# Decoder layer on one core: the scan result turned by VectorE blocks and a DRAM scratch, and three passes moved

## The chip, the cores and the metric

The kernel runs on one core of a Trainium2 chip. The metric is the device time of one execution in microseconds. TensorE (PE) multiplies matrices into PSUM, VectorE (DVE) and ScalarE (ACT) do elementwise work, GpSimd (POOL) shares elementwise work, and SyncE (SP) issues DMAs. Each engine works through its own queue in order and waits on semaphores.

## The reference

A post-norm decoder layer for 16 batches of 256 rows and 512 channels:

```python
x = layernorm(x + attention(x))              # 16 heads of 32, low-rank updates in each projection
kv = ctx * ctx                               # k = v = ctx, per channel
r[t] = decay[head] * r[t - 1] + kv[t]        # linear recurrence over the rows
x = layernorm(x + x * r)
h = gelu(silu(bitlinear(x, w1, b1)))         # x quantised to 8 bits, w1 ternary, 512 -> 2048
h = layernorm_2048(h) * ln_g + ln_b
x = layernorm(x + bitlinear(h, w2, b2))      # h quantised, w2 ternary, 2048 -> 512
```

## The kernel before, in words

One body of the loop, `body(j)`, works on four batches at once: the attention of batch j, the LayerNorms 1 and 2 and the up-projection of batch j-1, the middle of the feed-forward of batch j-2, and the down-projection and last LayerNorm of batch j-3. `lead()` fills this pipeline, `drain()` empties it. The order on each engine is written out by hand in five `body(j)` functions, one for each engine; the semaphores count up per batch (`wait(eng, name, b, k)`). A batch has NT = 2 tiles of 128 rows (index q).

- Attention, for head groups c = 0 to 3: `qk` (PE), `qk_hi` (ScalarE, L670), `qk_lo` (VectorE, L979), `scores` (PE, L1358), `maxima` (VectorE, L962 to L972), `shiftT` (PE, L1367, and its copy on ScalarE, L677), `shifted` (PE, L1382, into the four banks of `wave`), `probs_of` (ScalarE, L655), `weighted` (PE), `attn_norm` (VectorE, L986 to L995), `attn_split` (GpSimd, L437 and L440).
- The o product (PE), `layernorm1_sum` (VectorE, L1021), `inverse_std1` (GpSimd), `normalise` (ScalarE, L693).
- The context is loaded with channels on partitions into `ctx_sb` (`load_ctx`, L310), squared on ScalarE (L686, `ctx_square`), and scanned along the rows on VectorE at the end of `body(j)` (`scan`, L1003, clamped by L1006).
- In the next body PE transposes the scan result back to rows on partitions: `r(j, q)`, four 128x128 transposes for each q into a PSUM bank (L1455). `layernorm2_sum` (L1029) reads that bank and the rows. `inverse_std2` and `x_rms` (GpSimd, L462 to L520) and `normalise` follow.
- `quantise_x` (VectorE, L1052 to L1072) and `xq_store` (ScalarE, L702) write `xq`; a DMA transpose (`transpose_x`, L326) makes `xqT`; PE multiplies it in eight products `f(j, u)` (L1467 and, for the bias, L1468) into three banks in turn: `f(j, 3)` takes the bank of `f(j, 0)`, and waits until `silu` (ScalarE, L717) has read it. `gelu` (L723), `h_var` (L733), `h_rstd` (GpSimd) and `h_norm` (L738) follow.
- `g_mul` (GpSimd, L547) multiplies a 128x2048 tile by ln_g, `z_add` (VectorE, L1085) adds ln_b, `z_max` (L1090), `z_square` (ScalarE, L748), `z_rms` (GpSimd, L554, L557), `quantise_z` (VectorE, L1108 to L1117), `zq_store` (ScalarE, L708).
- A DMA transpose (`transpose_z`, L334) makes `hqT`; PE multiplies it in `y(j, q)` (L1474), `layernorm3_sum` (VectorE, L1130), `inverse_std3` (GpSimd, L482 to L487), `normalise`, and `store_out` (L319).

The order on PE around the change is `y(j,1)`, `shiftT(j,2)`, `r(j,0)`, `r(j,1)`, `shifted(j,2)`, `qk(j+1,0)`, `scores(j,3)`, `weighted(j,2)`, and later `qk(j+1,1)`, `f(j,0)` to `f(j,3)`, `shiftT(j+1,0)`, `f(j,4)` to `f(j,7)`. SP's queue in `body(j)` is `load_xT(j+1)`, `transpose_z(j-3,1)`, `store_out(j-3,0)`, `load_ctx(j)`, `transpose_x(j-1)`, `store_out(j-3,1)`, `transpose_z(j-2,0)`, `load_rows(j)`; before `load_ctx(j)` it waits for both r products of batch j-1. GpSimd's row passes `res1` (L496) and `res2` (L505) open its body, `res1` waiting for `load_rows`.

Of the kernel before, what the change touches and what calls it, by code (L numbers as in the profile page):

```python
# [15 lines left out]
P = 128  # L16
# [28 lines left out]
NROWS = 3  # L45


def decoder_kernel(nc, x, xT, ctxT, W, L, bq, bk, bv, bo, decay, w1T, b1, ln_g, ln_b, w2T, b2, out):
    b1_scratch = nc.dram_tensor("b1_scratch", (NPART, INNER), BF16, kind="Internal").ap()

    with ExitStack() as ctx:
# [68 lines left out]
        def sem(name):  # L120
# [40 lines left out]
            (PE, "shiftT_ready", 4), (PE, "pv_ready", 4), (PE, "o_ready", 2), (PE, "rT_ready", 2),  # L161
# [9 lines left out]
            (DV, "scan_done", 5), (DV, "ln1", 6), (DV, "ln2", 6), (DV, "x_quant", 14),  # L171
# [4 lines left out]
            (PO, "rstd2", 4), (PO, "rstd3", 6), (PO, "x_rms", 4), (PO, "h_stat", 8), (PO, "g_mul", 2),  # L176
# [3 lines left out]
            (SP, "xqT_loaded", 16), (SP, "hqT_loaded", 64),  # L180
        ]
# [24 lines left out]

        def rows_of(b):
# [10 lines left out]
        drain_bank = {("o", LAST, 0): 7, ("o", LAST, 1): 6, ("r", LAST, 0): 2, ("r", LAST, 1): 3,  # L218
# [7 lines left out]
        def drain_hqT(b, q):  # L226

            if b == PRIOR and q == 0:
                return hqT[:, :, :]
            if b == LAST and q == 1:  # L230
                t = v_sb[PRIOR % 2][:, :, :].rearrange("p q d -> p (q d)").bitcast(BF16)
            else:
                t = probs[:, LAST - b if b == PRIOR else 0, :, :].rearrange("p i t -> p (i t)").bitcast(BF16)
            return t.rearrange("p (k t) -> p k t", t=P)

# [19 lines left out]

        def flat(t):
            return t.rearrange("p a b -> p (a b)")
# [14 lines left out]
        def _(sp):  # L272
# [83 lines left out]
            def body(j):  # L356
                if alive(j, -1):
                    load_xT(j + 1)
                if alive(j, 3):
                    transpose_z(j - 3, 1)  # L360
                    store_out(j - 3, 0)
                load_ctx(j)
                transpose_x(j - 1)
                if alive(j, 3):
                    store_out(j - 3, 1)
                if alive(j, 2):
                    transpose_z(j - 2, 0)
                load_rows(j)
# [15 lines left out]
            def drain():  # L384
                transpose_z(THIRD, 1)
                transpose_x(LAST)
                store_out(THIRD, 0)
                store_out(THIRD, 1)
                transpose_z(PRIOR, 0)
                drain_transpose(PRIOR, 1)  # L390
                drain_transpose(LAST, 0)
                drain_transpose(LAST, 1)
                store_out(PRIOR, 0)
                store_out(PRIOR, 1)
                store_out(LAST, 0)
                store_out(LAST, 1)
# [10 lines left out]
        def _(po):  # L407
# [140 lines left out]

            def z_rms(b, q):
# [22 lines left out]
            def body(j):  # L572
# [70 lines left out]
        def _(ac):  # L643
# [162 lines left out]
            def body(j):  # L806
# [58 lines left out]
                if alive(j, 2):  # L865
                    z_square(j - 2, 1)
# [8 lines left out]
                if alive(j, 2):  # L875
                    zq_store(j - 2, 0)
# [66 lines left out]
        def _(dv):  # L943
# [53 lines left out]
            def scan(b):  # L997
# [4 lines left out]
                for c in range(KC):  # L1002
# [4 lines left out]
                                 ALU.max).then_inc(S["scan_done"], 1)  # L1007

# [66 lines left out]
            def z_add(b, q):  # L1075

                if b < PRIOR:
                    wait(dv, "g_mul", b, q + 1)
# [134 lines left out]
            def body(j):  # L1213
# [99 lines left out]
        def _(pe):  # L1313
# [135 lines left out]
            def r(j, q):  # L1449

                r_product(take(j, "r", q, "scan_done", j - 1, 5), q)

            def r_product(p, q):
                for kc in range(KC):
                    last = pe.transpose(p[:, kc * P:(kc + 1) * P], ctx_sb[:, kc, q * P:(q + 1) * P], ident[:, :])  # L1455
                last.then_inc(S["rT_ready"], 1)

# [44 lines left out]
            def drain():  # L1502
# [4 lines left out]
                wait(pe, "scan_done", LAST, 5)  # L1507
                for q in range(NT):
                    r_product(bank_of("r", q, LAST), q)
# [9 lines left out]
                drain_f(6, "ln2", LAST, 1)  # L1519
                drain_f(7, "ln2", LAST, 4)  # L1520
# [70 lines left out]
            def body(j):  # L1591
# [37 lines left out]
                if alive(j, 0):  # L1629
# [12 lines left out]
                if alive(j, 0):  # L1642
                    shifted(j, 3)
                if alive(j, -1):
# [69 lines left out]
```

## Time and profile before

| what | value |
|---|---|
| median of three runs | 1053.93 us (1052.6 to 1054.92) |
| the profiled execution's own time | 1050.39 us |
| its span, first to last instruction | 1048.6 us |
| mean granted TensorE clock | 0.962 of full speed |
| PE busy | 950.2 us, 91% of the span |
| DVE busy | 891.9 us, 85% |
| ACT busy | 827.4 us, 79% |
| POOL busy | 605.4 us, 58% |
| DMA, mean | 70 GB/s |

The span is what lies between the first and the last instruction; 1.8 us of the profiled execution's time lie around it. Busy shares are means over the lead, the loop and the drain. In the loop the granted clock is at full speed; in the last tenth of the span it falls to six to eight tenths. Line numbers (L1130) are those of the kernel before.

### The profile page before, as it was taken

To read this page: it belongs to the slowest core of one execution; us is meant where nothing else is said; L and a number is where in the kernel's file an instruction comes from. 1 tells how busy PE (TensorE), PEld (TensorE's weight loads), DVE (VectorE), ACT (ScalarE), POOL (GpSimd) and SP (SyncE) were. 2 spreads that over 40 slices of the span, in tenths; PEclk is the share of its full clock that TensorE was granted. 3 is DMA by queue.
4 is the path that set the end of the run, shared out by engine and by line. 5 is a ranking of instruction groups with operands and counts; after the bars stand their busy time and mean duration, and the time that the engine had idled before them with its cause. 6 is when DMAs were issued, how large, how long until landed. Compare 5 with 4: busy or idle time off the path is not lost.

```text
span 1048.6 us, 23525 instructions
## 1 busy us (share of the span) xinstructions
PE 950.2 (91%) x9388; PEld 655.1 (62%) x9388; DVE 891.9 (85%) x1474; ACT 827.4 (79%) x957; POOL 605.4 (58%) x767
## 2 busy tenths in 40 slices
PE   5998997999999999999999999999999999978416
PEld 3766756676767767676767767676767677644102
DVE  4577868989898999989898989899898989995766
ACT  3646686888979797988888797978889797977684
POOL 2332337474766749485757658494757566572653
PEclk9999998999999999999999999999999999988668
DMA  9432200213122121323131121323231321122213
GB/s 357 158 111 113 72 3 21 74 52 84 23 71 61 43 76 52 84 52 83 35 100 23 56 68 44 83 52 84 52 84 21 79 56 54 42 52 63 53 30 91
DMA packets 106352, 73.68 MB, mean 70 GB/s; under 512 B 91386, under 2 KB 91386, under 8 KB 104451
## 3 DMA queue, kind: packets, MB, share of 16 engines
q1 hardware_dynamic: 105522, 70.34, 24.2%
q8 instruction: 75, 1.23, 0.5%
q10 hardware_dynamic: 720, 1.84, 0.5%
q14 instruction: 35, 0.28, 0.1%
HBM read 41.73 MB, written 8.40 MB: 48 GB/s over the span
## 4 chain that ended last, share of the span: by engine, by line
PE 60%; DVE 26%; DMA 6%; ACT 4%; issue 3%; POOL 1%; SPq 0%; POOLq 0%; DVEq 0%; ACTq 0%
PE bank L1333 21%; PE bank L1467 11%; PE bank L1474 9%; DMA xqT<-xq 5%; PE wave L1382 4%; PE bank L1396 4%; PE wave L1358 3%; DVE neg_max L962 3%; DVE h L1085 3%; PE bank L1400 3%; DVE stats L1013 3%; PE bank L1468 3%; DVE fz L1090 2%; DVE rows L1029 2%; DVE qx L1052 1%
## 5 line engine op out<-in xcount | busy, mean ns | idle before, releaser
L962 DVE TENSOR_REDUCE neg_max<-wave 128x8 f32<-128x2048 f32 x64 | 146.2, 2284 | 39.0 <-PE wave L1358 39.0
L547 POOL TENSOR_TENSOR h<-h,g_tile 128x2048 f32<-128x2048 f32 x30 | 139.9, 4663 | 39.1 <-ACT h L738 39.1
L655 ACT ACTIVATE probs<-wave 128x1024 f32<-128x1024 f32 x128 | 124.4, 1024 | 40.5 <-PE wave L1382 40.3
L1467 PE MATMUL bank<-w,xqT 128*128 128x512 fp8e4 x496 | 129.7, 384 | 20.6 <-DMA xqT<-xq 20.6
L437 POOL TENSOR_SCALAR attn_hi<-attn 128x256 fp32r<-128x256 f32 x64 | 31.8, 497 | 150.1 <-DVE attn L995 134.8
L717 ACT ACTIVATE h<-bank,qx 128x512 f32<-128x512 f32 x124 | 83.8, 689 | 24.4 <-PE bank L1468 22.1
L693 ACT ACTIVATE rows<-rows,rstd 128x512 f32<-128x512 f32 x96 | 74.3, 807 | 33.1 <-POOL rstd L453 18.5
L1085 DVE TENSOR_TENSOR h<-h,b_tile 128x2048 f32<-128x2048 f32 x32 | 84.0, 2624 | 17.0 <-POOL h L547 16.9
L1467 PEld LDWEIGHTS bank<-w,xqT 128*128 128x128 bf16 x496 | 47.8, 99 | 78.0 <-issue 17.4
L1474 PE MATMUL bank<-w,hqT 128*128 128x512 fp8e4 x416 | 94.3, 380 | 0.0
L496 POOL TENSOR_TENSOR rows<-rows,bo_tile 128x512 f32<-128x512 f32 x32 | 52.6, 1665 | 71.2 <-DMA rows<-x 71.2
L1003 DVE TENSOR_TENSOR_SCAN ctx_sb<-decay_col,ctx_sb 128x256 f32<-128x256 f32 x64 | 78.8, 1290 | 0.0
L1333 PE MATMUL bank<-xT_hi,wq_hi 128*128 128x256 f32 x256 | 78.4, 306 | 0.1
L440 POOL TENSOR_TENSOR attn_lo<-attn,attn_hi 128x256 fp32r<-128x256 f32 x64 | 73.7, 1151 | 5.3
L1382 PE MATMUL wave<-qk_parts 32*128 32x256 f32 x1536 | 73.4, 301 | 3.6 <-ACT shift_rows L677 3.6
L670 ACT ACTIVATE qk_parts<-bank,bias_qk 128x256 fp32r<-128x256 f32 x128 | 53.6, 474 | 25.9 <-PE bank L1333 25.9
L1396 PE MATMUL bank<-probs,v_sb 128*32 128x256 f32 x1024 | 70.6, 394 | 3.1 <-ACT probs L655 2.1
L1333 PE MATMUL bank<-xT_lo,wq_hi 128*128 128x256 f32 x256 | 73.3, 286 | 0.0
L1333 PE MATMUL bank<-xT_hi,wq_lo 128*128 128x256 f32 x256 | 73.2, 286 | 0.0
L738 ACT ACTIVATE h<-h,fs 128x2048 f32<-128x2048 f32 x32 | 66.8, 2089 | 7.8 <-POOL fs L538 7.8
L1358 PE MATMUL wave<-qk_parts 32*128 32x256 f32 x1536 | 63.7, 296 | 10.1 <-ACT probs L655 8.0
L1382 PEld LDWEIGHTS wave<-qk_parts 32*128 32x128 f32 x1536 | 56.9, 190 | 25.0 <-issue 20.1
(181 smaller groups left out, 2844.1 us busy)
## 6 DMA issues: line engine op xcount, KB each, us to landing
ctx_sb<-ctxT SPq DMA_DIRECT2D x16, 512.0 KB, 3.8
rows<-x SPq DMA_DIRECT2D x16, 512.0 KB, 4.0
out<-rows SPq DMA_DIRECT2D x32, 256.0 KB, 2.5
xT_in<-xT SPq DMA_DIRECT2D x15, 512.0 KB, 4.7
h<-w1T SPq DMA_DIRECT2D x4, 1024.0 KB, 14.6
h<-w2T SPq DMA_DIRECT2D x4, 1024.0 KB, 4.8
h<-Wq SPq DMA_DIRECT2D x1, 1024.0 KB, 6.2
h<-Wk SPq DMA_DIRECT2D x1, 1024.0 KB, 9.8
```

Of the source, the lines that this page charges most:

```text
L547: po.tensor_tensor(h_of(b, q)[:, :], h_of(b, q)[:, :], g_tile[:, :], ALU.mult).then_inc(done, 1)
L655: ac.activation(probs[:, kt, :, :], wave[:, :, kt * T:(kt + 1) * T], ACT.Exp, scale=SM_SCALE).then_inc(S["probs_ready"], 1)
L717: ac.activation(h_of(b, q)[:, n * FW:(n + 1) * FW], bank_of("f", u, b), ACT.Silu, scale=qx[:, X_DEQ, q:q + 1]).then_inc(S["silu_done"], 1)
L962: dv.tensor_reduce(neg_max[:, :, :], wave[:, :, :].rearrange("p j (t k) -> p j t k", t=NT), axis=AX_X, op=ALU.max, negate=True).then_inc(S ...
L1003: dv.tensor_tensor_scan(ctx_sb[:, c, :], decay_col[:, c:c + 1].to_broadcast([P, T]), ctx_sb[:, c, :], 0.0, ALU.mult, ALU.add).then_inc(S[" ...
L1085: dv.tensor_tensor(h_of(b, q)[:, :], h_of(b, q)[:, :], b_tile[:, :], ALU.add).then_inc(S["z_added"], 1)
L1333: last = pe.matmul(psum, lhsT, rhs, start=(first and i == 0), stop=(final and i == len(pairs) - 1))
L1358: last = pe.matmul(bank[head][:, qt * T:(qt + 1) * T], parts[at, qp, qt * P:(qt + 1) * P], parts[at, kp, :], start=(i == 0), stop=(i == 2))
L1382: last = pe.matmul(bank[head][:, kt * T:(kt + 1) * T], keys, queries, start=(i == 0), stop=(i == 3))
L1396: pe.matmul(bank[4][i * HD:(i + 1) * HD, 0:T], v_sb[b % 2][:, kt, ch:ch + HD], probs[:, kt, i, :], start=(kt == 0), stop=(kt == NT - 1))
L1467: pe.matmul(p[:, :], xqT[:, q, kc, :], w1[:, kc, n * FW:(n + 1) * FW], start=(kc == 0), stop=False)
L1474: last = pe.matmul(p[:, :], hqT[:, k, :], w2[:, k, :], start=(k == 0), stop=(k == FC - 1))
```

## The change

The scan result is no longer transposed on PE. VectorE turns its 32x32 blocks from `ctx_sb` into `x_round` by two transposes of 128x512 at the end of `scan`, and `move_state` on SP stores this to a DRAM scratch and loads it back into `ctx_sb` in four parts, so that rows stand on partitions. The host lays out the context and the decay so that the channels come out in order. `layernorm2_sum` reads `ctx_sb` instead of a PSUM bank; `load_ctx` waits for it. The second `g_mul` of a batch is split into two halves, each of which awaits a step of VectorE. `z_add(j-2, 1)` moves behind `quantise_x(j-1)`, and `z_square(j-2, 1)` behind `ctx_square(j)`. In the drain the f products 6 and 7 no longer wait for LayerNorm 2's sum.

```diff
+    state_scratch = nc.dram_tensor("state_scratch", (SB, HD, SB, NT * D // SB), F32, kind="Internal").ap()
...
-                 ("r", 0, 1, "ln2", 1), ("r", 1, 1, "ln2", 4), ("v", 0, -1, "v_stored", 1),
-                 ("v", 1, -1, "v_stored", 2)]
+                 ("v", 0, -1, "v_stored", 1), ("v", 1, -1, "v_stored", 2)]
...
             def load_ctx(b):
-                wait(sp, "rT_ready", b - 1, 2)
+                wait(sp, "ln2", b - 1, 4)
...
+            def move_state(b):
+
+                wait(sp, "scan_done", b, 7)
+                wait(sp, "state_moved", b - 1, 16 * SB)
+                sp.dma_start(state_scratch.rearrange("a i s x -> (a i) (s x)"),
+                             state_blocks).then_inc(S["state_out"], 16)
+                wait(sp, "state_out", b, 16)
+                for s in range(SB):
+                    to = state_rows[s * HD:(s + 1) * HD, :].rearrange("p (a x) -> p a x", a=SB)
+                    sp.dma_start(to, state_scratch[:, :, s, :].rearrange("a i x -> i a x")
+                                 ).then_inc(S["state_moved"], 16)
...
             def body(j):
                 if alive(j, -1):
                     load_xT(j + 1)
+                move_state(j - 1)
...
             def drain():
+                move_state(LAST)
...
+            def g_mul_half(b, i):
+
+                wait(po, "h_normed", b, 2)
+                if b == 0:
+                    po.wait_ge(u_gain, 16 * 2)
+                cols = slice(i * INNER // 2, (i + 1) * INNER // 2)
+                half = h_of(b, 1)[:, cols]
+                po.tensor_tensor(half, half, g_tile[:, cols], ALU.mult).then_inc(S["g_mul"], 1)
...
                 if alive(j, 2):
-                    g_mul(j - 2, 1)
+                    wait(po, "ln2", j - 1, 6)
+                    g_mul_half(j - 2, 0)
                 if alive(j, 1):
                     inverse_std2(j - 1)
                     x_rms(j - 1)
+                if alive(j, 2):
+                    wait(po, "shift_split", j, 8)
+                    g_mul_half(j - 2, 1)
...
-                if alive(j, 2):
-                    z_square(j - 2, 1)
                 if alive(j, 1):
                     xq_store(j - 1)
...
                 if alive(j, 0):
                     ctx_square(j)
                 if alive(j, 2):
+                    z_square(j - 2, 1)
                     zq_store(j - 2, 0)
...
+                wait(dv, "scan_done", b, KC + 1)
+                wait(dv, "xq_stored", b - 1, 1)
+                blocks = state_blocks.rearrange("p (s q k c) -> p q k s c", s=SB, q=NT, c=HD)
+                for q in range(NT):
+                    dv.transpose(blocks[:, q, :, :, :],
+                                 ctx_sb[:, :, q * P:(q + 1) * P].rearrange("p k (s c) -> p k s c", c=HD)
+                                 ).then_inc(S["scan_done"], 1)
...
             def layernorm2_sum(b, q):
-                wait(dv, "rT_ready", b, q + 1)
+                wait(dv, "state_moved", b, 16 * SB)
                 wait(dv, "norm1", b, q + 1)
-                dv.scalar_tensor_tensor(rows_of(b)[:, q, :], bank_of("r", q, b), SCAN_SCALE, rows_of(b)[:, q, :],
-                                        ALU.add, ALU.mult).then_inc(S["ln2"], 1)
+                state = state_rows.rearrange("p (a q x) -> p q a x", a=SB, q=NT)[:, q, :, :]
+                x_rows = rows_of(b)[:, q, :].rearrange("p (a x) -> p a x", a=SB)
+                dv.scalar_tensor_tensor(x_rows, state, SCAN_SCALE, x_rows, ALU.add, ALU.mult).then_inc(S["ln2"], 1)
...
-                if alive(j, 2):
-                    z_add(j - 2, 1)
                 if alive(j, 1):
                     quantise_x(j - 1)
                 if alive(j, 2):
+                    z_add(j - 2, 1)
                     quantise_z(j - 2, 0)
...
-                if alive(j, 1):
-                    r(j, 0)
-                    if j == 1:
-                        pe.wait_ge(u_scale, 5)
-                    r(j, 1)
...
-                drain_f(6, "ln2", LAST, 1)
-                drain_f(7, "ln2", LAST, 4)
+                drain_f(6, "probs_ready", LAST, 8)
+                drain_f(7, "probs_ready", LAST, 8)
```

## Rows read from the trace of the kernel before

**Rows 1.** Chain of waits, two bodies: start us, us, what

```profile
578.40 0.76 DVE rows L1130
...
597.17 3.39 DMA xqT<-xq
...
636.51 0.76 DVE rows L1130
```

**Rows 2.** TensorE in order of time: start us, us; bracketed, idle before

```profile
578.42 0.60 PE L1455 MATMUL bank<-ident,ctx_sb 128*128 128x128 f32 x4
...
579.79 0.63 PE L1382 MATMUL wave<-qk_parts 32*128 32x256 f32 x12
...
600.70 1.02 PE L1467 MATMUL bank<-w,xqT 128*128 128x512 fp8e4 x4 [0.75 <-DMA xqT<-xq]
...
603.93 1.03 PE L1467 MATMUL bank<-w,xqT 128*128 128x512 fp8e4 x4
```

**Rows 3.** ScalarE in order of time, the same body

```profile
579.01 0.36 ACT L677 ACTIVATE shift_rows<-wave 128x256 fp32r<-128x256 f32 x1
...
599.49 2.00 ACT L708 ACTIVATE h<-h,neg_round 128x2048 bf16<-128x2048 f32 x1 [0.41 <-DVE h L1117]
...
602.81 2.01 ACT L717 ACTIVATE h<-bank,qx 128x512 f32<-128x512 f32 x3
```

**Rows 4.** Two VectorE lines, whole span: ns min/median/max, first and last start

```profile
L990 DVE STREAM_TRANSPOSE inverse<-inverse_T x64: 445/445/447, 47.4 to 947.6; 128x256 f32<-128x256 f32 x64
...
L1003 DVE TENSOR_TENSOR_SCAN ctx_sb<-decay_col,ctx_sb x64: 658/1692/1783, 85.2 to 955.0; 128x256 f32<-128x256 f32 x64
```

**Rows 5.** VectorE in order of time, the same body and the next

```profile
590.21 2.28 DVE L1085 TENSOR_TENSOR h<-h,b_tile 128x2048 f32<-128x2048 f32 x1
...
593.85 0.60 DVE L1056 TENSOR_SCALAR qx<-qx 128x2 f32<-128x2 f32 x1
594.48 0.17 DVE L1057 RECIPROCAL qx<-qx 128x2 f32<-128x2 f32 x1
...
598.17 1.29 DVE L1117 TENSOR_SCALAR h<-h,fz 128x2048 f32<-128x2048 f32 x1
...
610.61 5.58 DVE L1003 TENSOR_TENSOR_SCAN ctx_sb<-decay_col,ctx_sb 128x256 f32<-128x256 f32 x4
...
616.83 0.74 DVE L1130 SCALAR_TENSOR_TENSOR rows<-bank,fz,rows 128x512 f32<-128x512 f32 x1
...
620.97 2.29 DVE L962 TENSOR_REDUCE neg_max<-wave 128x8 f32<-128x2048 f32 x1 [0.92 <-PE wave L1358]
...
628.96 2.48 DVE L1085 TENSOR_TENSOR h<-h,b_tile 128x2048 f32<-128x2048 f32 x1 [1.32 <-POOL h L547]
```

**Rows 6.** GpSimd in order of time, the same body and the next

```profile
580.23 4.67 POOL L547 TENSOR_TENSOR h<-h,g_tile 128x2048 f32<-128x2048 f32 x1
...
588.11 0.72 POOL L520 TENSOR_TENSOR qx<-qx,neg_half 128x2 f32<-128x2 f32 x1
...
618.60 0.19 POOL L482 TENSOR_SCALAR rstd<-mean_var 128x1 f32<-128x1 f32 x1 [2.43 <-DVE mean_var L1015]
```

**Rows 7.** SP's queue in order of time

```profile
604.18 0.58 SPq L314 DMA_DIRECT2D rows<-x  x1
...
626.91 2.60 SPq L334 DMA_TRANSPOSE hqT<-h  x2
```

**Rows 8.** The page's DMA issues: KB each, us to landing

```profile
rows<-x SPq DMA_DIRECT2D x16, 512.0 KB, 4.0
```

**Rows 9.** Chain of waits, first body and drain

```profile
107.97 1.70 PE bank L1455 x8
...
964.92 0.87 PE wave L1455 x8
```

**Rows 10.** ScalarE and TensorE in order of time, drain

```profile
950.58 0.69 ACT L717 ACTIVATE h<-bank,qx 128x512 f32<-128x512 f32 x1 [0.25 <-PE bank L1468]
...
952.80 1.03 PE L1467 MATMUL bank<-w,xqT 128*128 128x512 fp8e4 x4
```

More of the change, by code:

```diff
@@ L45 @@
 NROWS = 3
+SB = P // HD
 def decoder_kernel(nc, x, xT, ctxT, W, L, bq, bk, bv, bo, decay, w1T, b1, ln_g, ln_b, w2T, b2, out):
     b1_scratch = nc.dram_tensor("b1_scratch", (NPART, INNER), BF16, kind="Internal").ap()
+    state_scratch = nc.dram_tensor("state_scratch", (SB, HD, SB, NT * D // SB), F32, kind="Internal").ap()
     with ExitStack() as ctx:
@@ L160, in decoder_kernel @@
             (PE, "shifted_ready", 4), (PE, "scores_ready", 4), (PE, "qk_ready", 4), (PE, "v_ready", 2),
-            (PE, "shiftT_ready", 4), (PE, "pv_ready", 4), (PE, "o_ready", 2), (PE, "rT_ready", 2),
+            (PE, "shiftT_ready", 4), (PE, "pv_ready", 4), (PE, "o_ready", 2),
             (PE, "f_ready", 8), (PE, "y_ready", 2),
@@ L170, in decoder_kernel @@
             (DV, "qk_lo", 8), (DV, "max_done", 4), (DV, "shift_split", 8), (DV, "inverted", 12), (DV, "attn_done", 4),
-            (DV, "scan_done", 5), (DV, "ln1", 6), (DV, "ln2", 6), (DV, "x_quant", 14),
+            (DV, "scan_done", 7), (DV, "ln1", 6), (DV, "ln2", 6), (DV, "x_quant", 14),
             (DV, "z_added", 4), (DV, "z_quant", 12),
@@ L175, in decoder_kernel @@
             (PO, "x_lo", 1), (PO, "attn_split", 8), (PO, "res1", 2), (PO, "res2", 2), (PO, "rstd1", 3),
-            (PO, "rstd2", 4), (PO, "rstd3", 6), (PO, "x_rms", 4), (PO, "h_stat", 8), (PO, "g_mul", 2),
+            (PO, "rstd2", 4), (PO, "rstd3", 6), (PO, "x_rms", 4), (PO, "h_stat", 8), (PO, "g_mul", 3),
             (PO, "z_rms", 4),
@@ L180, in decoder_kernel @@
             (SP, "xqT_loaded", 16), (SP, "hqT_loaded", 64),
+            (SP, "state_out", 16), (SP, "state_moved", 16 * SB),
         ]
@@ L205, in half_rows, with flat @@
             return t.rearrange("p (i k) -> p i k", i=2)[:, :, 0:INNER // 2]
+        def flat(t):
+            return t.rearrange("p a b -> p (a b)")
         def rows_of(b):
@@ L217, in decoder_kernel @@
         LAST, PRIOR, THIRD = NB - 1, NB - 2, NB - 3
-        drain_bank = {("o", LAST, 0): 7, ("o", LAST, 1): 6, ("r", LAST, 0): 2, ("r", LAST, 1): 3,
+        drain_bank = {("o", LAST, 0): 7, ("o", LAST, 1): 6,
                       ("y", THIRD, 0): 0, ("y", THIRD, 1): 1, ("y", PRIOR, 0): 4, ("y", PRIOR, 1): 5,
@@ L234, in drain_hqT @@
             return t.rearrange("p (k t) -> p k t", t=P)
+        state_blocks = flat(x_round[:, :, :])
+        state_rows = flat(ctx_sb[:, :, :])
         def fz_of(b):
@@ L254, in ffw @@
             return h[FFW_BUFFER[n]][:, :]
-        def flat(t):
-            return t.rearrange("p a b -> p (a b)")
         def merge_bank(m, kc):
@@ L1077, in z_add @@
                 if b < PRIOR:
-                    wait(dv, "g_mul", b, q + 1)
+                    wait(dv, "g_mul", b, 1 if q == 0 else 3)
                 elif q == 0:
@@ L1447, in o_second_half @@
                 split_product(bank_of("o", q, j - 1)[:, :], o_terms(q, (2, 3)), first=False).then_inc(S["o_ready"], 1)
[L1449 to L1456, printed above, removed]
             def f(j, u):
@@ L1506, in drain @@
                 wait(pe, "probs_ready", LAST, 8)
-                wait(pe, "scan_done", LAST, 5)
-                for q in range(NT):
-                    r_product(bank_of("r", q, LAST), q)
                 drain_y(THIRD, 0)
@@ L1643, in body @@
                     shifted(j, 3)
+                if j == 1:
+                    pe.wait_ge(u_scale, 5)
                 if alive(j, -1):
@@ L1685 @@
     put("xT", channels_first(a["x"]))
-    put("ctxT", channels_first(a["ctx_2048"]))
+    put("ctxT", a["ctx_2048"].reshape(NB, T, GH, KC, HD).transpose(0, 2, 4, 3, 1).reshape(NB, P, KC, T))
     for n in "qkvo":
@@ L1695 @@
     put("bo", a["L0_attn_bo"].reshape(1, D))
-    put("decay", a["L0_xattn_decay"].reshape(NG, GH).T)
+    put("decay", a["L0_xattn_decay"].reshape(GH, KC))
     put("w1T", a["L0_ffn_w1"].T.reshape(KC, P, INNER).transpose(1, 0, 2))
```

1 line of the change is left out of this document (removed).

## The prediction

> **What bounds the kernel now.** I read the page first: PE is busy 91% of the span and at full clock, VectorE 85%. That alone would say "take work off PE, gain it all". The chain of waits says otherwise, so I read it next, for two periods of the steady loop [rows 1]. One body is 636.51 - 578.40 = 58.1 us, and its chain has three parts. From the first f product at 600.70 [rows 2] it stays on PE to the end of the second y product, which lets go VectorE's L1130 at 636.51: 35.8 us. From L1130 (578.40) it stays on VectorE until `quantise_x` ends, 18.8 us. Then the DMA transpose of xq takes 3.4 us, and PE starts the next f. PE work that stands between the y product and the f products is not on that chain; the eight transposes of `r` stand exactly there. The reader should see in [rows 1] that PE's 91% is partly work done while waiting for VectorE's string.
>
> Then PE in order of time [rows 2], ScalarE [rows 3], VectorE [rows 5] and GpSimd [rows 6] in that body. VectorE has few holes; the two that matter are 0.92 us at L962, which waits for PE, and 1.32 at L1085, which waits for GpSimd. Next I asked which chain is second, because a change that shortens the first is worth only the distance to it.
>
> **The transposes of r leave PE.** From their first, 578.42, to `shifted` at 579.79 is 1.37 us [rows 2]. But `shifted(j,2)` needs ScalarE's copy of the shift, 579.01 + 0.36 = 579.37 [rows 3], queued there behind a normalisation. With about 0.1 us for the handover it could begin at 579.5: of 1.37 us some 0.3 is won, and the rest becomes a wait for ScalarE. `scores(j,3)` and what follows are then held by VectorE's line from L1130 anyway. So this part is worth 0.3 us on PE here and nothing on the present chain; without ScalarE's wait it would be 1.37.
>
> **z_add behind quantise_x.** The second ln_b pass, 2.28 us, leaves the chain's VectorE part [rows 5]. xq is ready that much sooner, and f would start at 598.4 + 0.1 if PE were there. PE isn't: f starts at 600.70 with 0.75 us of waiting, so less the 0.3 above it reaches f near 599.7, 1 us sooner. Is this 1 us kept? The fourth f product (603.93) [rows 2] reuses the bank of the first and waits for the first Silu. The Silus start at 602.81 behind a table load, behind `zq_store` at 599.49 [rows 3], which waits for L1117, ending at 598.17 + 1.29 = 599.46 [rows 5]. The order before L1117 is turned round but its sum is the same, the 2.28 us included. On ScalarE, `z_square(j-2,1)` now waits for z_add's new end (L1117's start less the five short steps before it, about 597.1); its pass over the tile takes about the 2.00 us of `zq_store`'s over the same, so it ends near 599.3, just when L1117 does, and four shorter instructions are done ahead of it. So the Silu stays at 602.81, its result at about 603.5, the fourth f at 603.6 instead of 603.93: of 1 us only **0.3 us per body** is kept. The new chain is L1130, VectorE 21.1 us to L1117, ScalarE 4.0 us, PE.
>
> **Two block transposes on VectorE.** The trace has no 128x512 one. L990 turns 128x256 in 0.445 us [rows 4]: doubled it is 0.89, the upper bound; a fixed part of 0.17, which L1057 takes for two elements [rows 5], leaves 0.27 for 256 elements and makes 0.71 for 512. The lower bound is a quarter of L1085's 2.28 us for 2048, 0.57. I take 0.71, since L1130's 0.74 for 512 elements is nearest: 1.4 us per body for two. They stand after the scan and before L1130 at 616.83, where VectorE is late already. Followed on: L1130, L1021 and their statistics move by 1.4 less what the loop gained before. The scan gains less than 0.3, since it shares its time with GpSimd's four row passes, whose start hangs on a load issued behind `zq_store`: 0.2. So they move by 1.2 us; the 0.92 us before L962 takes most of it, and the shift reaches PE 0.2 us late compared with PE's own arrival. The GpSimd side: L482 at 618.60 [rows 6] moves by 1.2 too, and the next small instructions, which lead to ScalarE's normalisation, GpSimd's L547 at 624.26 and VectorE's L1085 at 628.96, become about 0.1 us later than today. VectorE's later L1130 thus comes 0.1 sooner than today, not 0.3: **0.2 given back**. Net -0.1 us per body. With 0.89 each it is +0.3.
>
> The Trainium skill (VectorE: DVE Perf Modes, The three transpose paths) lists VectorE's 128x128 bf16 block transpose at 311 ns against TensorE's 390. An estimate by that page, four times 311 ns for 128x512, would be 1.24 us each and put the body at about +1.0 us. L990's 0.445 us for 128x256 f32 [rows 4] disagrees, being less than twice 311, and I go by the row.
>
> **GpSimd's pass in two halves.** L547 (4.67 us at 580.23) becomes two of 2.33 us. The first awaits ln2's statistics, the second the shift split and the small instructions that today end at 588.11 + 0.72 [rows 6], moved by 0.6. The second half thus runs about 589.5 to 591.8; queued behind it are `inverse_std3`, `z_rms` and `attn_split(j,2)`, whose reader, VectorE's last attn product, stands behind L1117 (599.46) and is far off. What matters is the meeting with VectorE. A scan instruction takes 0.658 us undisturbed and 1.692 in the median [rows 4], and L1056 0.60 where nothing in it is work for more than 0.17 [rows 5]: while GpSimd reads large tiles, a VectorE instruction with two SBUF inputs waits for its end. In after, L1055 meets the second half (0 to 0.4 us), z_add meets attn_lo (0 to 0.3), and L1029, which now reads both operands in SBUF, meets attn_lo before 580.23 (0 to 0.24). Against that, today's stall of 0.4 in L1055 or L1056 goes. Bounds -0.4 to +0.5 per body; I take +0.1, between them.
>
> The Trainium skill (SBUF — State Buffer, Who interferes with whom) has the rule: a VectorE instruction with two SBUF inputs and a GpSimd one that reads SBUF exclude each other for the whole instruction. The two scan times agree [rows 4]. It speaks against `layernorm2_sum` reading SBUF in place of PSUM, and for the waits put before the halves.
>
> **The DRAM round trip.** `move_state` stands in SP's queue behind `load_xT` and ahead of `transpose_z(j-3,1)`, issued at 626.91 [rows 7]; the scan's result is ready at 618.2. A 512 KB load takes 4.0 us from issue to landing [rows 8], and its issue 0.58 [rows 7]; the first for the store, then four issues of at most 0.6, gives SP free at 624.7, 2.2 us before it is needed. The reloads land by about 629, and the reader, which comes after L1130 at 636.51, waits for nothing. `load_ctx` waits for the second ln2 sum instead of r, some 2.5 us later, and its reader `ctx_square` stands on ScalarE just before 599.49. Cost nothing; if a DMA took over 6.2 us, the z transpose would be late, and past another 1.3 us the y product.
>
> **The ends.** In the first body the r transposes stand on the chain with 1.70 us [rows 9]; less ScalarE's copy, 0.36 and handover, 1.2 us go. In the last body VectorE and ScalarE stop holding xq: the fourth f starts at 952.80, and the first Silu, which could run at 950.33, would end at 951.0, so f moves by 1.7 us [rows 10]. In the drain the eight transposes, 0.87 us, lie on the chain [rows 9]. The drain's own `move_state` starts near the last f product, and its reader needs LayerNorm 1 of the o products, which end at 964.92: I count it covered, with 1 us in doubt. Sum 3.8 us.
>
> **Sum.** Twelve full bodies: 12 x (-0.3 + 0.2 + 0.1) = 0, and -3.8 at the ends. The profiled execution is 1050.39 us (span 1048.6), so 1046.6; the runs' median is 1053.93, 3.5 above the profiled one, and from there it is **1050.1 us**, -0.36%.
>
> **Rivals.** (A) As said, bodies within -0.1 and +0.1: 1048.9 to 1051.4. Chance 0.38. (B) VectorE becomes the loop's bound: its transposes cost 0.89 each, or the port meetings come out at +0.5. That is +0.35 to +0.6 per body, +4 to +7 less 3.8: 1054 to 1057. It decides from 0.32 us per body. For it: VectorE is busy 85% even with both ends counted. Against: the 1.32 us before L1085 can absorb some. Chance 0.25, half of it beyond 0.2%. (C) The stalls mostly go: the halves meet nothing, and L1055/L1056 run free; then the loop follows ScalarE and GpSimd, at -0.3 to -0.9 per body: 1039 to 1046.5. For it: z_add's wait of 1.32 us shows VectorE isn't saturated. Against: the 21.1 us string holds the Silus. Chance 0.22. (D) SP's queue is late by the round trip, and y waits 0.5 to 1.5 us per body: 1056 to 1068. Against: 2.2 + 1.3 us of room. Chance 0.07. (E) The freed 1.37 + 0.75 us are kept in full, PE-bound, 2 us per body: 1026. Against: both other strings. Chance 0.03. (F) With its blocks scattered, the transpose pays each element twice, 0.17 + 2 x 0.54 = 1.25 us each, +1.1 per body: 1063. Against: L990's pace. Chance 0.05.
>
> A change under 0.2% (2.1 us) can't be told from none. Faster: most of A, C and E, 0.55; same: the rest of A and half of B, 0.18; slower 0.27. The likeliest case's own range is 1048.5 to 1051.8; the eight-in-ten range leaves out E, the bottom of C and the top of D: 1042 to 1059.
>
> **What the profile after should show.** PE's busy time falls by 128 transposes, while idle appears before `shifted(j,2)` (ScalarE) and before the fourth f (Silu); the wait for xqT is gone or moved; two STREAM_TRANSPOSE of about 0.7 us; no wait at L962 for PE; SP free before the z transpose. Wrong if the transposes exceed 0.9 us, if L1055 or L1029 grow by over 0.4, or if the y product waits for hqT.

## The result, and the profile after

The changed kernel takes **1063.95 us** in the median of 5 runs (1060.19 to 1065.19), beside 1053.93 us for the kernel before (5 runs, 1052.6 to 1055.32): a ratio of 1.0086, 95% interval 1.0060 to 1.0111. The ratio is taken over all the runs; the quotient of two medians differs from it by up to 0.2%, here and in the table below. The changed kernel is slower by 0.9%; the prediction was 1050.1, range 1042 to 1059. Run once more on another chip it had 1.0083 (1.0063 to 1.0104), so the loss belongs to the kernel. It isn't the clock: from 300 to 860 us of the span the granted clock is 1.00 in both.

First the page of the changed kernel: the span, the busy times and the chain that ended last.

```profile
span 1063.2 us, 23435 instructions
...
PE 941.3 (89%) x9260; PEld 638.7 (60%) x9260; DVE 924.0 (87%) x1506; ACT 827.6 (78%) x957; POOL 615.4 (58%) x781
...
DVE 48%; PE 17%; issue 13%; ACT 10%; POOL 9%; DMA 2%; SPq 0%; ACTq 0%; POOLq 0%; DVEq 0%
...
state_scratch<-x_round SPq DMA_DIRECT2D x16, 512.0 KB, 2.6
ctx_sb<-state_scratch SPq DMA_DIRECT2D x64, 128.0 KB, 2.8
```

The kernel before had PE 60% and VectorE 26% of that chain; now VectorE has 48% and PE 17%. PE did lose its work (9260 matmuls in place of 9388) and time with it, but no longer sets the end. The two last rows are the DRAM round trip, from issue to landing: 2.6 us out, 2.8 us back.

Then the chain of waits in one body of the steady loop, from the first short step of `quantise_z` (L1147) to the L1169 behind the next y product, which answers to [rows 1].

```profile
605.47 0.71 DVE fz L1147
...
607.04 1.30 DVE h L1156
...
608.39 2.00 issue
610.38 1.28 ACT L749
...
611.68 0.69 ACT h L749
...
612.42 1.04 PE bank L1496 x4
...
618.26 6.56 DVE ctx_sb L1034 x4
...
626.20 0.67 DVE x_round L1043
626.87 0.64 DVE rows L1169
...
633.12 4.67 POOL h L566
...
637.81 1.82 DVE h L1124
...
645.23 0.67 DVE rows L1169
```

It no longer waits for PE at L1169 (once L1130). It runs from VectorE to ScalarE and through a single PE piece, the fourth f product at 612.42. The bodies, from one `quantise_x` to the next, measure 58.85 us in the median of the loop, where the kernel before has 58.07: +0.78, which over twelve is 9.4 of the 10 us.

VectorE in order of time (start, duration, engine, line, operation), to lay beside [rows 5]: the layernorm2 sums, then the end of the string.

```profile
587.90 1.06 DVE L1069 SCALAR_TENSOR_TENSOR rows<-ctx_sb,rows 128x512 f32<-128x512 f32 x1
...
589.83 0.68 DVE L1069 SCALAR_TENSOR_TENSOR rows<-ctx_sb,rows 128x512 f32<-128x512 f32 x1
...
599.73 0.50 DVE L1094 TENSOR_TENSOR qx<-qx 128x2 f32<-128x2 f32 x1
```

```profile
603.26 2.29 DVE L1124 TENSOR_TENSOR h<-h,b_tile 128x2048 f32<-128x2048 f32 x1
605.47 0.70 DVE L1147 TENSOR_TENSOR fz<-fz 128x1 f32<-128x1 f32 x1
...
607.04 1.29 DVE L1156 TENSOR_SCALAR h<-h,fz 128x2048 f32<-128x2048 f32 x1
```

And GpSimd over the same stretch, which answers to [rows 6].

```profile
587.67 0.74 POOL L459 TENSOR_TENSOR attn_lo<-attn,attn_hi 128x256 fp32r<-128x256 f32 x1
591.53 2.40 POOL L575 TENSOR_TENSOR h<-h,g_tile 128x1024 f32<-128x1024 f32 x1 [3.12 <-DVE mean_var L1053]
...
597.79 2.42 POOL L575 TENSOR_TENSOR h<-h,g_tile 128x1024 f32<-128x1024 f32 x1
...
603.28 2.88 POOL L459 TENSOR_TENSOR attn_lo<-attn,attn_hi 128x256 fp32r<-128x256 f32 x1
```

Four meetings can be read off these two views. (1) The layernorm2 sum at 587.90 lasts 1.06 us, its twin at 589.83 only 0.68; `attn_lo` is on GpSimd from 587.67 to 588.41. (2) The first short instruction of `quantise_x`, L1094 at 599.73, lasts 0.50 and ends at 600.23, with GpSimd's second half of ln_g (600.21). (3) `attn_lo` at 603.28 lasts 2.88 us, 0.74 where it is free: it stands behind `z_add`, which began 0.02 us earlier. (4) `z_add` ends near 605.47, and the next VectorE instruction, L1147, takes 0.70 for a work of 0.16: it ends at 606.17, and `attn_lo` at 606.16. So the waiting GpSimd instruction seems to have gone first, and the short VectorE one behind it paid its length; the order is inferred from the two ends, and e3 below tests it.

The same over the whole loop, grouped by line and shape (count, then busy us and mean ns of one; after the second bar idle time before them): first after, then the kernel before. L1147 serves both tiles of a batch, one at 0.70 and one at 0.15 us, hence its mean of 425 ns; L1069 has one sum at 1.06 and one at 0.68.

```profile
L1069 DVE SCALAR_TENSOR_TENSOR rows<-ctx_sb,rows 128x512 f32<-128x512 f32 x22 | 18.8, 856 | 0.0
...
L1043 DVE STREAM_TRANSPOSE x_round<-ctx_sb 128x512 f32<-128x512 f32 x22 | 14.4, 691 | 0.4
...
L1147 DVE TENSOR_TENSOR fz<-fz 128x1 f32<-128x1 f32 x22 | 9.4, 425 | 0.0
...
L1094 DVE TENSOR_TENSOR qx<-qx 128x2 f32<-128x2 f32 x11 | 5.4, 491 | 0.4
```

```profile
L1029 DVE SCALAR_TENSOR_TENSOR rows<-bank,rows 128x512 f32<-128x512 f32 x22 | 14.9, 679 | 0.0
...
L1055 DVE TENSOR_TENSOR qx<-qx 128x2 f32<-128x2 f32 x12 | 4.4, 367 | 0.4
L1056 DVE TENSOR_SCALAR qx<-qx 128x2 f32<-128x2 f32 x12 | 4.2, 347 | 0.4
...
L1108 DVE TENSOR_TENSOR fz<-fz 128x1 f32<-128x1 f32 x23 | 3.6, 156 | 0.4
```

PE's waits, by time (the bracket is the idle time before the row, and what ended it): the shifted product, which answers to 579.79 in [rows 2], and the fourth f, which answers to 603.93.

```profile
587.57 0.63 PE L1420 MATMUL wave<-qk_parts 32*128 32x256 f32 x12 [1.22 <-ACT shift_rows L709]
```

```profile
612.42 1.04 PE L1496 MATMUL bank<-w,xqT 128*128 128x512 fp8e4 x4 [0.98 <-ACT h L749]
```

### The profile page after: what moved, and what is told of

Same layout as the page of the kernel before. It is cut to its first block, busy times and chain, and to the rows that moved or that the text cites. A ratio compares the mean times of both kernels' runs of the same rounds, so it can differ in the third digit from the quotient of the medians.

```text
span 1063.2 us, 23435 instructions
## 1 busy us (share of the span) xinstructions
PE 941.3 (89%) x9260; PEld 638.7 (60%) x9260; DVE 924.0 (87%) x1506; ACT 827.6 (78%) x957; POOL 615.4 (58%) x781
## 4 chain that ended last, share of the span: by engine, by line
DVE 48%; PE 17%; issue 13%; ACT 10%; POOL 9%; DMA 2%; SPq 0%; ACTq 0%; POOLq 0%; DVEq 0%
DVE ctx_sb L1034 7%; PE bank L1371 6%; DVE neg_max L993 6%; POOL h L566 5%; DVE stats L1051 4%; DVE h L1156 4%; PE bank L1496 3%; DVE qk_parts L1010 3%; DVE h L1124 3%; ACT h L770 3%; DVE rows L1069 2%; DVE qx L1091 2%; DVE rows L1169 2%; ACT L749 2%; DVE fz L1129 2%
## 5 line engine op out<-in xcount | busy, mean ns | idle before, releaser
L459 POOL TENSOR_TENSOR attn_lo<-attn,attn_hi 128x256 fp32r<-128x256 f32 x64 | 101.3, 1583 | 5.3
L515 POOL TENSOR_TENSOR rows<-rows,bo_tile 128x512 f32<-128x512 f32 x32 | 56.6, 1788 | 73.3 <-DMA rows<-x 73.3
L566 POOL TENSOR_TENSOR h<-h,g_tile 128x2048 f32<-128x2048 f32 x16 | 74.8, 4673 | 38.7 <-ACT h L770 38.7
L1420 PE MATMUL wave<-qk_parts 32*128 32x256 f32 x1536 | 74.6, 302 | 23.8 <-ACT shift_rows L709 23.3
L575 POOL TENSOR_TENSOR h<-h,g_tile 128x1024 f32<-128x1024 f32 x28 | 67.3, 2403 | 46.5 <-DVE mean_var L1053 43.2
L456 POOL TENSOR_SCALAR attn_hi<-attn 128x256 fp32r<-128x256 f32 x64 | 28.7, 449 | 111.8 <-DVE attn L1026 96.4
L1034 DVE TENSOR_TENSOR_SCAN ctx_sb<-decay_col,ctx_sb 128x256 f32<-128x256 f32 x64 | 89.4, 1456 | 0.0
```

Of the source, the lines that this page charges most:

```text
L459: po.tensor_tensor(attn_lo[:, c, :], attn[:, :], attn_hi[:, c, :].bitcast(F32), ALU.subtract).then_inc(S["attn_split"], 1)
L566: po.tensor_tensor(h_of(b, q)[:, :], h_of(b, q)[:, :], g_tile[:, :], ALU.mult).then_inc(done, 1)
L1034: dv.tensor_tensor_scan(ctx_sb[:, c, :], decay_col[:, c:c + 1].to_broadcast([P, T]), ctx_sb[:, c, :], 0.0, ALU.mult, ALU.add).then_inc(S[" ...
L1420: last = pe.matmul(bank[head][:, kt * T:(kt + 1) * T], keys, queries, start=(i == 0), stop=(i == 3))
```

## The experiments

Two theories were on record. **Theory 1**: the loop follows VectorE's string from the later y product's L1169 to `quantise_z`'s rounding, and meetings with GpSimd, in which an instruction of one engine is held until one of the other has ended, lengthen the string. **Theory 2**: VectorE is simply full, and the two block transposes' 1.4 us are the loss. Each run below is given by its body (`quantise_x` to `quantise_x`, median of the loop) and its string (start of the later L1130/L1169 to the end of the first L1117/L1156 behind it, median), both from its trace. The first four ran on one chip (kernel before there 1051.01 us), the next four on a second (1053.5), the last four on a third (1053.12).

| kernel | body | string | time | ratio to before (95%) |
|---|---|---|---|---|
| before | 58.07 | 21.06 | 1053.93 | 1 |
| after | 58.85 | 22.03 | 1063.95 | 1.0086 (1.0060, 1.0111) |
| e1, turn alone | 62.59 | 24.25 | 1111.31 | 1.0571 (1.0531, 1.0611) |
| e2, moves and halves | 58.35 | 21.67 | 1058.34 | 1.0051 (1.0032, 1.0071) |
| e3, after + split held | 58.21 | 21.39 | 1051.75 | 0.9999 (0.9980, 1.0018) |
| e4, after without the turn | 58.49 | 21.79 | 1056.51 | 1.0047 (1.0029, 1.0066) |
| e5, moves + split held | 57.35 | 20.63 | 1040.25 | 0.9881 (0.9861, 0.9900) |
| e6, after with one pass | 62.24 | 24.24 | 1109.5 | 1.0534 (1.0518, 1.0550) |
| e7, e3 + second split behind | 59.00 | 22.18 | 1063.32 | 1.0095 (1.0081, 1.0109) |
| e8, e3 without the turn | 57.84 | 21.12 | 1047.76 | 0.9945 (0.9933, 0.9958) |
| e9, moves alone | 57.89 | 21.20 | 1048.23 | 0.9965 (0.9950, 0.9980) |
| e10, split held alone | 57.68 | 20.64 | 1048.8 | 0.9961 (0.9947, 0.9975) |
| e11, e5 + halves | 57.70 | 21.02 | 1047.09 | 0.9955 (0.9940, 0.9971) |
| e12, after again | 58.84 | 22.02 | 1061.36 | 1.0083 (1.0063, 1.0104) |

**e1, the turn alone.** The changed kernel with the two moves and the halves undone: on GpSimd `g_mul(j - 2, 1)` stands where the kernel before has it, on VectorE `z_add(j - 2, 1)` ahead of `quantise_x(j - 1)`, on ScalarE `z_square(j - 2, 1)` ahead of `xq_store(j - 1)`, as in the kernel before (ScalarE's lines are not printed).

```
# GpSimd, in the changed kernel
-                    wait(po, "ln2", j - 1, 6)
-                    g_mul_half(j - 2, 0)
+                    g_mul(j - 2, 1)
...
-                if alive(j, 2):
-                    wait(po, "shift_split", j, 8)
-                    g_mul_half(j - 2, 1)
# VectorE
+                if alive(j, 2):
+                    z_add(j - 2, 1)
                 if alive(j, 1):
                     quantise_x(j - 1)
                 if alive(j, 2):
-                    z_add(j - 2, 1)
                     quantise_z(j - 2, 0)
```

> The changed kernel with the two moves and the halves undone: the scan result still goes by VectorE's blocks and DRAM, GpSimd's second ln_g pass is one 4.67 us instruction in its old place, z_add and z_square stand where they stood. Theory 1 (the body is set by VectorE's string from L1130 (L1169 after) to the quantising passes, and GpSimd's port meetings lengthen it): layernorm2_sum now has two SBUF inputs and meets the whole ln_g pass, which starts at the same moment; 3.2 to 4.4 us of stall on the string, a body of 61 to 62.5 us, 1090 to 1107 us. Theory 2 (VectorE is simply full, and the two block transposes' 1.4 us per body are the loss): the body is 58.1 to 59.2 us, 1054 to 1068 us, and the sum instruction stays near 0.7 us.

Measured: body 62.59, 0.1 over theory 1's range, and 1111.31 us, 4 over it. VectorE and GpSimd of that kernel in order of time:

```profile
608.77 0.80 DVE L1066 SCALAR_TENSOR_TENSOR rows<-ctx_sb,rows 128x512 f32<-128x512 f32 x1
...
610.43 4.22 DVE L1066 SCALAR_TENSOR_TENSOR rows<-ctx_sb,rows 128x512 f32<-128x512 f32 x1
```

```profile
608.28 0.74 POOL L459 TENSOR_TENSOR attn_lo<-attn,attn_hi 128x256 fp32r<-128x256 f32 x1
608.98 5.11 POOL L566 TENSOR_TENSOR h<-h,g_tile 128x2048 f32<-128x2048 f32 x1
```

The second sum takes 4.22 us for a work of 0.68, because GpSimd's one pass of ln_g runs to 614.09. In the kernel before the same pass lies over the same sums [rows 6] and costs them nothing, 679 ns of mean above: there the sum reads PSUM. Reading the state from SBUF is what makes it pay. Theory 2's price for this kernel, 1.4 us of transposes, is far off the 4.5 us measured.

The string's part of these 4.5 us is 3.19. The way from its end to the fourth f product is 5.36 us, 0.89 longer than before, because here PE is late too: it waits for VectorE's shift, and runs slower behind that wait.

```profile
620.43 0.69 PE L1403 MATMUL wave<-ident,shift 128*128 128x128 f32 x2 [3.64 <-DVE shift L1000]
```

From 620 to 624 us the granted clock is 0.61. Over 300 to 860 us of the span it is 0.96 in e1, and in e6 too, where the kernels before and after have 1.00. So part of the loss of these two kernels is the lower clock behind PE's wait; how much was not separated.

**e2, the moves and the halves, r on TensorE.** The square moves on ScalarE too; its lines are not printed.

```
# GpSimd, in the kernel before
-                    g_mul(j - 2, 1)
+                    wait(po, "ln2", j - 1, 6)
+                    g_mul_half(j - 2, 0)
...
+                if alive(j, 2):
+                    wait(po, "shift_split", j, 8)
+                    g_mul_half(j - 2, 1)
# VectorE, before quantise_z(j - 2, 0)
-                if alive(j, 2):
-                    z_add(j - 2, 1)
                 if alive(j, 1):
                     quantise_x(j - 1)
                 if alive(j, 2):
+                    z_add(j - 2, 1)
```

> The kernel before with the two moves and the awaited halves alone: r stays on PE, no block transposes, no DRAM trip, layernorm2_sum reads PSUM. Theory 1: the stall of the first step of quantise_z behind z_add (0.54 us) stays, the 0.4 us at layernorm2_sum goes, and the meeting of quantise_x with the second half stays (0.34): a body of 58.2 to 58.5 us, 1053 to 1057 us. Theory 2: with the transposes gone the moves give their forecast gain, a body of 57.8 us, 1047 to 1050 us.

Measured 58.35, as theory 1 said; the time, 1058.34 us, is 1.3 over its range. Without any block transpose the loop is 0.28 us longer than before, with L1120 (the first short step of `quantise_z`) at 0.69 and L1067 (of `quantise_x`) at 0.50. Theory 2 has no room for that. From here to after, the turn adds the other 0.50 us a body.

**e3, the third attention split held.** The one meeting nobody had priced, L1147's, is taken away by holding the split back until `quantise_z`'s short steps are done:

```
                 if alive(j, 0):
+                    if alive(j, 2):
+                        wait(po, "z_quant", j - 2, 5)
                     attn_split(j, 2)
                     attn_split(j, 3)
```

> The changed kernel with one wait more: attn_split(j,2) on GpSimd waits until quantise_z's fifth small step of batch j-2 is done, so attn_lo no longer queues behind z_add and in front of quantise_z. Theory 1: the first step of quantise_z falls from 0.70 to 0.16 us, the body from 58.85 to 58.3 us, 1056 to 1059 us. Theory 2: nothing changes within 0.2 us per body, 1062 to 1065 us.

Measured 58.21; its L1149 (L1147 in after) is back at 0.15. Of after's 0.78 us a body, 0.64 is gone with one wait on GpSimd, and all of VectorE's work still there. The time is equal to before, and 4 us under theory 1's range: twelve bodies of -0.64 are 7.7 of the 12 us between the medians of after and e3, which ran on different chips.

**e4, without the turn.** Both `dv.transpose` are left out, so the scan's result is stored and reloaded unturned and the sum adds other numbers.

```
-                for q in range(NT):
-                    dv.transpose(blocks[:, q, :, :, :],
...
-                                 ).then_inc(S["scan_done"], 1)
```

> The changed kernel without the two VectorE block transposes (left out: the scan result is stored and reloaded unturned, so that part of the computation is missing). Theory 1: 1.37 us of VectorE work per body go, but they lie where VectorE has room against ScalarE and GpSimd; the string from the second y product on is untouched: a body of 58.5 to 58.7 us, 1059 to 1062 us. Theory 2: the loss goes with them: 58.0 us or less, 1050 to 1054 us.

Measured 58.49: 1.38 us less work on VectorE shortens the body by 0.36, the string by 0.24 (the first layernorm2 sum meets the split for less long, about 0.80 in place of 1.06; the mean of both sums is 0.74 in place of 0.86). The time, 1056.51 us, is 2.5 under theory 1's range. Theory 2 fails.

**e5, moves and held split, without turn and halves.** What is left of the change when its costly half is taken off: e2's lines on VectorE, the square's move on ScalarE and e3's lines on GpSimd, in the kernel before.

> The kernel before with the ln_b pass and its square moved behind quantised x, and GpSimd's third attention split held until the five short steps of quantise_z have run; r stays on TensorE, GpSimd's second ln_g pass stays one. Theory 1 (the loop is set by VectorE's string from the second y product to quantise_z, and meetings at the port lengthen it): the string keeps its 21.1 us and its short step before quantise_z's rounding stays at 0.15, so the prediction's own 0.3 us a body is won: body 57.6 to 57.9, time 1046 to 1049 beside a kernel before of 1051. Theory 2 (VectorE is simply full): no work leaves VectorE, body 58.1, 1050 to 1052.

Measured 57.35 and **1040.25 us**, below the lower end: theory 1 had the sign, but not the stall of 0.43 us in L1056 of the kernel before [rows 5]. That one was the same split, `attn_lo`, which the wait moves away too; the string went to 20.63. In the kernel before L1056 runs from 593.85 to 594.45 [rows 5], and GpSimd has

```profile
593.65 0.77 POOL L440 TENSOR_TENSOR attn_lo<-attn,attn_hi 128x256 fp32r<-128x256 f32 x1
```

which ends at 594.42. (In the other half of the bodies the stall falls on L1055.) Twelve bodies of -0.72 are 8.6 of the 13.25 us between the medians; the first body, 63.53 us where before has 65.71, holds 2.2 more. The chain of waits of this kernel:

```profile
570.54 3.57 PE bank L1474 x16
...
574.14 0.76 DVE rows L1131
...
574.94 0.66 PE bank L1455 x4
575.60 1.15 PE wave L1382 x27
...
592.68 3.01 PE bank L1333 x24
595.69 0.88 PE bank L1467 x4
```

```profile
core 0: us, PE busy (x) PEld busy (x) DVE busy (x) ACT busy (x) POOL busy (x), PEclk, DMA share, GB/s
300.00:860.00 560.00, 557.63 (x5659) 387.73 (x5670) 512.45 (x870) 484.10 (x568) 355.20 (x452) 1.00 0.25 62
```

It is PE from end to end, 557.63 us busy of 560 at full clock, but for 0.8 us at L1131. Here the transposes at 574.94 are on the chain, 0.66 us, and here a cheaper way to turn the state might win up to that much a body; it was not tried.

**e6, one pass of ln_g again, moves and turn kept.** e1's lines on GpSimd alone.

> The changed kernel with GpSimd's second ln_g pass in one piece again; both moves and the turn by VectorE stay. Theory 1: the one pass of 4.67 us stands over the layernorm2 sum as it did in the kernel with the turn alone (4.18 us where 0.68 is free), string near 24 to 25, body 61.5 to 62.8, 1098 to 1112. Theory 2: halves have nothing to do with VectorE's load, body 58.8, 1062 to 1065.

Measured 62.24, the second sum at 4.18 as in e1. So the halves are a repair that only the turn needs.

**e7, the second split behind the first half,** on top of e3:

```
-                if alive(j, 0):
-                    attn_split(j, 1)
                 if alive(j, 2):
                     wait(po, "ln2", j - 1, 6)
                     g_mul_half(j - 2, 0)
+                if alive(j, 0):
+                    attn_split(j, 1)
```

> The version with the third attention split held (body 58.21), and with the second attention split put behind the first half of ln_g, so that it no longer stands over the first layernorm2 sum. Theory 1: that sum falls from 0.94 to 1.06 back to 0.68, the string by 0.3 to 0.4, body 57.8 to 57.95, 1046 to 1049 beside 1051; unless the later split itself is waited for by TensorE, which then would show as idle time at its scatter product. Theory 2: body stays at 58.2, 1051 to 1053.

Neither theory's number came: 59.00, and 1063.32 us. The sum fell to 0.68 as theory 1 said, and the price came back with interest elsewhere. VectorE and GpSimd:

```profile
596.69 1.22 DVE L1093 TENSOR_REDUCE qx<-rows 128x2 f32<-128x1024 f32 x1 [0.53 <-ACT rows L727]
597.95 1.05 DVE L1096 TENSOR_TENSOR qx<-qx 128x2 f32<-128x2 f32 x1
```

```profile
591.51 0.40 POOL L456 TENSOR_SCALAR attn_hi<-attn 128x256 fp32r<-128x256 f32 x1
592.00 0.73 POOL L459 TENSOR_TENSOR attn_lo<-attn,attn_hi 128x256 fp32r<-128x256 f32 x1
...
596.59 2.39 POOL L575 TENSOR_TENSOR h<-h,g_tile 128x1024 f32<-128x1024 f32 x1
```

The split, 1.2 us with its `attn_hi`, now delays GpSimd's small instructions, with them ScalarE's normalisation (VectorE idles 0.53 us for it) and the second half of ln_g, so that L1096 lies 1.05 us under it. A meeting moved is not a meeting removed.

**e8, e3 without the turn.** e4's edit and e3's together; it leaves out the same part.

> The version with the third attention split held (body 58.21), without the two block transposes: the scan's result goes out and comes back unturned, so that the sum adds other numbers of the same size. Theory 1 (the 1.4 us stand before a hole of VectorE and are mostly absorbed, 0.2 to 0.36 kept): body 57.85 to 58.0, 1047 to 1049. Theory 2 (VectorE full): the whole 1.35 is won, body 56.9, 1035 to 1037.

Measured 57.84: with the meeting gone too, the 1.38 us of transposes are worth 0.37. Theory 2's 56.9 is far off.

**e9 to e11, the parts one by one.** e9 is the kernel before with the two moves only (e2's lines on VectorE, and the square on ScalarE), e10 with e3's wait only, e11 is e5 with e2's lines on GpSimd.

> The kernel before with the ln_b pass and its square moved behind quantised x, and nothing else. Theory 1: the short instruction of quantise_x that meets the third attention split keeps its stall of 0.43 us, so the string is 21.05 us where the version with the split held had 20.63 and a body of 57.35; body 57.6 to 57.85, 1043 to 1047. If the whole gain came from the hold, body 58.0 and 1051 to 1054; if it all came from the move, 57.35 and 1040.

> The kernel before with only the third attention split held until quantise_z's short steps have run. Theory 1: the stall of 0.43 us in quantise_x's second short instruction goes, it stands on the chain, nothing else changes: string 20.63, body 57.65, 1047 to 1049. If the stall was covered, body 58.07 and 1051 to 1054.

> The fast version (both moves, third attention split held, r on TensorE) with GpSimd's second ln_g pass in two awaited halves as in the change. Theory 1: the second half stands over quantise_x's first short instruction, 0.5 where 0.16 is free, string 20.95 to 21.0 where one pass has 20.63; body 57.5 to 57.8, 1042 to 1046. If the halves cost nothing, 57.35 and 1040; the distance from there to the version that also turns r on VectorE (58.21) is then what the turn costs.

e9: 57.89 and 1048.23 us, both just above the range. The string is 21.20, since L1054 meets the split, 0.71 to 0.74 for 0.16, in more than half of the bodies. The move is worth 0.18 a body while that meeting stays. e10: 57.68, 1048.8 us, as expected. e11: 57.70 as expected; the second half over `quantise_x` (0.49 for 0.16) costs 0.35 against e5. Its time, 1047.09, is a microsecond over the range given. From e11 to e3 (58.21) the turn alone is added: 0.51 us a body, where from e2 to after it is 0.50. Of these 0.51, e8 gives 0.37 to the two transposes and leaves 0.14 to the rest, above all the sum that reads SBUF.

**e12, the changed kernel again.**

> The changed kernel as it is, once more, beside the others on one chip: body 58.85, 1061 to 1065, ratio to the kernel before 1.007 to 1.011; it says whether that result belongs to a chip or to the kernel.

Body 58.84, ratio 1.0083: as before.

## Why the prediction was wrong

It forecast no change per body and 3.8 us less at the ends; it measured +0.78 per body and nothing gained at the ends. Its steps:

- **The string stays 21.1 us, port meetings +0.1, "bounds -0.4 to +0.5": this is the step that failed.** The string measured 22.03, +0.97, outside its own bounds. Part by part, in the body shown: today's stall went, -0.43, as said; the meeting with the second half came, +0.34 (0 to 0.4 had been said); `z_add` +0.01 (0 to 0.3); the layernorm2 sum L1069 +0.38, 0.14 over its bound of 0.24; 0.12 in `quantise_x`'s other short steps; and **L1147 +0.54, which had been put at nothing: the sum has no term for it**. The four terms that the sum has come to +0.30, inside its bounds. The prediction saw that `z_add` would meet `attn_lo`, and asked only how much longer `z_add` would get. It did not get longer: the split waited for it, then delayed the next VectorE instruction. e3 shows the size (-0.64 a body when only this goes). e1 and e6 show the second cost, the sum with both operands in SBUF, at 4.2 us.
- **"Of 1 us only 0.3 us per body is kept" on the way through ScalarE**: right. From the string's end to the fourth f product it was 603.93 - 599.46 = 4.47 us before [rows 2, 5] and is 612.42 - 608.33 = 4.09, -0.38. The median is 4.09 in e2, e5, e9 and e11 too, which have the move without the turn.
- **"0.2 given back" by the transposes**: about right here, but not all of their price. From the fourth f product to the next L1169 before the string it was 32.58 and is 32.76; e4 and e8, without the transposes, have 32.62 and 32.63, so 0.12 or so is theirs. Together 0.97 - 0.38 + 0.18 = 0.77, the body's +0.78. The term "the scan gains less than 0.3" was wrong: its 44 instructions in the loop took 61.4 us before and 71.0 after, 0.87 more a body. e2 has 71.0 as well, so this comes with the moves and the halves. VectorE's room before `maxima`, its waits for PE at L962, was 11.1 us in the loop before, is 8.5 in e2 and 0.0 in after.
- **The transposes' 0.71 each**: 0.69 measured. The estimate of 1.24 from the Trainium skill (VectorE: DVE Perf Modes, The three transpose paths) and rival F's 1.25 were far off. F's time, 1063, is the measured one by coincidence. e4 and e8 price both at 0.36 and 0.37 a body, not at 1.4; the rest is absorbed by VectorE's holes, as said, but more than 0.2 comes through: some 0.25 of it in the string, where the later VectorE lets the first layernorm2 sum meet the split for longer, which had no term.
- **What TensorE gives up is worth nothing on the chain**: right in the loop, and for the reason given. PE waits 1.22 us for ScalarE's copy before the shifted product and 0.98 for the Silu before the fourth f.
- **The DRAM round trip costs nothing**: right. SP's own queue shows the store, the four reloads and, long after them, the z transpose, so rival D was out:

```profile
568.04 0.33 SPq L321 DMA_DIRECT2D state_scratch<-x_round  x1
570.67 1.75 SPq L326 DMA_DIRECT2D ctx_sb<-state_scratch  x4
576.55 3.22 SPq L351 DMA_TRANSPOSE hqT<-h  x2
```

- **The ends' -3.8**: the first body is shorter by 1.4 (65.71 us before, 64.29 after, 64.46 in e12), where 1.2 had been said. That is luck at least in part, since the reason given, r off TensorE, isn't shown: e2 and e9 keep r on TensorE and have 64.03 and 63.87, so the moves give it alone. The last body and the drain gave nothing: the last `quantise_x` distance is 40.9 before and 44.35 and 42.1 in the two executions of after; over all kernels it lies between 40.85 and 44.35, with r on TensorE or off it. From the last `quantise_x` to the end it is 67.3 us before, 68.1 and 67.5 after, so the 0.87 us of the drain's transposes didn't show either. From the first f product to the first o product of that body it was 10.98 us before, and is 13.72 after and 12.02 in e12. In after PE waits 0.78 and 1.25 us in it (962.71 and 965.21), and the granted clock is 0.79 from 965.2 to 973.3; before it is 0.70 for 4.6 us and then 1.00. How much is waiting and how much the lower clock behind it was not separated.

Rival B had the right sign and engine ("the port meetings come out at +0.5"), at 0.25, and stopped at 1057, because it took +0.5 as the most the meetings could cost. What moved the forecast to the wrong side was a mean between bounds: each meeting was priced by chance, 0 to so much, although the order on both engines is fixed and the trace of before gives both sides' starts to 0.1 us. The meeting at quantised z could have been found by placing the third `attn_split` behind the second half of ln_g, which the prediction itself did; it ended at "is far off" for its reader and did not ask what it would stand over.

The Trainium skill (SBUF — State Buffer, Who interferes with whom) was named for a two-input VectorE instruction and a GpSimd read shutting each other out, and it spoke against the layernorm2 sum in SBUF. The runs agree, 4.22 us for 0.68 in e1, and 0.68 where the operand is in PSUM. The prediction gave that rule at most 0.24 us at the sum. It also read the 0.60 us of L1056 as an instruction with two SBUF inputs; L1056 is a TENSOR_SCALAR with one, so the sentence cited doesn't cover it. What the runs show of it is that it ends with `attn_lo`, and that e10, which holds the split, has it at 0.17.

## What to carry to other kernels

Before moving a tile from PSUM to SBUF as an operand of a two-input VectorE instruction, lay GpSimd's order of time beside VectorE's: a GpSimd pass over that instruction can hold it until the pass ends (3.5 us in e1), and a repair (passes cut and awaited) can move the collision to the next short instruction (e7, e11). When a long VectorE instruction holds GpSimd off, look for the cost one instruction later. And try the cheap parts of a change alone: here the move of one addition with its square, and one wait on GpSimd, gave -1.19% (e5). The part that looked like the gain, 128 transposes off TensorE, took it all back (e3: 0.9999): 0.35 us a body for the halves that it needs, 0.51 for the turn itself.

## What the runs showed of the hardware

- A GpSimd instruction held by a long two-input VectorE one delays the VectorE instruction queued directly behind that: in after, `attn_lo` takes 2.88 us for 0.74 and L1147 0.70 for 0.16, ending together (606.16 and 606.17); in e3, where the split comes later, the same step takes 0.15.
- A VectorE instruction of 128x2 can pay the whole rest of a GpSimd pass: 1.05 us for 0.16 in e7, over a 2.39 us half (ends 599.00 and 598.98). One with a single input pays too: L1056 before, 0.60 for 0.17.
- VectorE's block transpose of 128x512 f32 with scattered 32x32 blocks takes 0.69 us; two plain ones of 128x256 would be 0.89 [rows 4].
- One wait on GpSimd (e10) is worth 0.39 us a body on a kernel whose page shows GpSimd 58% busy.
- In e1 PE waits 3.64 us, and the granted clock is 0.61 from 620 to 624 us, behind that wait.
